# Gated cross-attention block on one core: the first projection of each attention unit in front of the denominators

## What is computed

```python
x = x + tanh(g_xattn[0]) * xattn(layernorm(x), ctx, w_q, w_k, w_v, w_o)
x = x + tanh(g_ffn[0])   * ffn(layernorm(x), gate_w, gate_up_w, down_w)

def xattn(query, kv, w_q, w_k, w_v, w_o):      # 16 heads of 8
    q, k, v = query @ w_q.T, kv @ w_k.T, kv @ w_v.T          # split into heads
    attn = softmax(einsum('bqhd,bkhd->bhqk', q, k) * 8 ** -0.5)
    return einsum('bhqk,bkhd->bqhd', attn, v) @ w_o.T

def ffn(x, gate_w, gate_up_w, down_w):         # 8 experts of 512, the best 2 of each token weighted
    ...
```

## Time and profile before

| | |
|---|---|
| three timed runs | 300.0, 299.88, 297.85 us, median 299.88 |
| profiled execution | 299.23 us |
| its span, first to last instruction | 297.5 us |
| PE busy | 284.7 us, 96% |
| DVE busy | 220.0 us, 74% |
| ACT busy | 181.3 us, 61% |
| POOL busy | 102.5 us, 34% |
| granted TensorE clock | 1.00 |

### The profile page before, as it was taken

The page is one execution under the profiler, slowest core; times in us unless marked ns, Lnnn a source line. Parts: engine busy times, 40 slices in busy tenths (PEclk is TensorE's granted clock), DMA queues, the critical chain, the costliest instruction groups (busy, mean ns, idle before and its releaser), DMA issues.

```text
span 297.5 us, 8034 instructions
## 1 busy us (share of the span) xinstructions
PE 284.7 (96%) x2826; PEld 218.9 (74%) x2826; DVE 220.0 (74%) x420; ACT 181.3 (61%) x370; POOL 102.5 (34%) x113
## 2 busy tenths in 40 slices
PE   7988999999999999999999999999889998998994
PEld 3464867876886886786787688887688887887862
DVE  4688878678786786777867878677256988888861
ACT  1635677676667757766767666557528775666500
POOL 4598423114015113312311411024500464776300
PEclk9999999999999999999999999999999999999999
DMA  7397960991792595298097079600000000000001
GB/s 249 88 203 196 220 194 16 209 249 54 162 264 96 103 218 197 52 220 248 0 218 198 0 156 240 237 0 2 2 2 0 1 2 0 0 1 0 0 0 31
DMA packets 9924, 32.19 MB, mean 108 GB/s; under 512 B 2576, under 2 KB 3088, under 8 KB 9904
## 3 DMA queue, kind: packets, MB, share of 16 engines
q1 hardware_dynamic: 9472, 31.60, 41.9%
q10 hardware_dynamic: 432, 0.33, 0.3%
HBM read 13.26 MB, written 0.23 MB: 45 GB/s over the span
## 4 chain that ended last, share of the span: by engine, by line
PE 86%; DVE 7%; issue 3%; ACT 2%; DMA 1%; SPq 0%; DVEq 0%; POOL 0%; ACTq 0%
PE score_ps L927 17%; PE max_ps L947 14%; PE o_ps L961 14%; PE misc_ps L915 7%; PE misc_ps L909 5%; PE score_ps L1190 3%; PE score_ps L1191 3%; PE score_ps L1192 3%; PE max_ps L977 3%; PE o_ps L1272 2%; PE misc_ps L999 2%; DVE part_max L687 2%; PE score_ps L909 2%; PE max_ps L970 1%; PE misc_ps L1106 1%
## 5 line engine op out<-in xcount | busy, mean ns | idle before, releaser
L687 DVE TENSOR_REDUCE part_max<-max_ps 112x1 f32<-112x512 f32 (+1 forms) x192 | 118.5, 670 | 40.4 <-PE max_ps L947 38.2
L510 ACT ACTIVATE probs<-score_ps 128x448 f32<-128x448 f32 x192 | 92.0, 543 | 28.9 <-PE score_ps L927 27.2
L947 PE MATMUL max_ps<-kx,qx 96*112 96x512 f32 (+1 forms) x192 | 77.5, 410 | 2.0 <-DVE part_max L687 0.9
L927 PEld LDWEIGHTS score_ps<-qx,kx 104*128 104x128 f32 (+1 forms) x384 | 66.5, 187 | 15.0 <-issue 7.9
L927 PE MATMUL score_ps<-qx,kx 104*128 104x224 f32 (+1 forms) x384 | 76.9, 285 | 0.5 <-ACT probs L510 0.4
L362 POOL TENSOR_TENSOR k_low<-k_full,k_high 128x512 fp32r<-128x512 f32 (+1 forms) x21 | 26.3, 1256 | 67.6 <-ACT k_full L493 67.3
L961 PE MATMUL o_ps<-probs,v_sb 128*32 128x112 f32 (+1 forms) x1536 | 47.6, 262 | 1.0 <-ACT probs L510 1.0
L961 PEld LDWEIGHTS o_ps<-probs,v_sb 128*32 128x32 f32 (+1 forms) x1536 | 36.1, 109 | 13.2 <-ACT probs L510 6.1
L947 PEld LDWEIGHTS max_ps<-kx,qx 96*112 96x112 f32 x192 | 33.8, 177 | 6.6 <-issue 2.9
L422 POOL TENSOR_TENSOR kx<-gu_sb,kx 128x512 fp32r<-128x512 f32 x16 | 23.0, 1440 | 30.6 <-ACT kx L590 30.4
L505 ACT ACTIVATE v_sb<-misc_ps 128x512 f32<-128x512 f32 x24 | 14.4, 601 | 20.0 <-PE misc_ps L915 20.0
(11 more groups left out here) (177 smaller groups left out, 376.7 us busy)
## 6 DMA issues: line engine op xcount, KB each, us to landing
kx<-k_high SPq DMA_DIRECT2D x60, 187.5 KB, 3.9
kx<-k_low SPq DMA_DIRECT2D x30, 187.5 KB, 3.9
ctx_sb<-in_ctxT SPq DMA_DIRECT2D x7, 750.0 KB, 6.1
gu_sb<-in_guT SPq DMA_DIRECT2D x8, 512.0 KB, 4.7
dn_sb<-in_dnT SPq DMA_DIRECT2D x8, 256.0 KB, 5.1
ctx_sb<-in_ctxT SPq DMA_DIRECT2D x2, 256.0 KB, 4.1
kx<-k_high SPq DMA_DIRECT2D x4, 123.5 KB, 2.3
kx<-k_high SPq DMA_DIRECT2D x4, 64.0 KB, 2.0
```

Source lines behind the costliest of these rows:

```text
L510: nc.scalar.activation(probs[:, (KT * h + t) % 8, :], score_ps[:, t % 3, 0:SC // 2], ACT.Exp, scale=SCALE).then_inc(exp_done, 1)
L687: nc.vector.reduce_max(part_max[:, p, c:c + 1], max_ps[0:PC, bank, 0:size], AX.X).then_inc(max_taken, turns)
L927: last = nc.tensor.matmul(score_ps[0:m, t % 3, GC * g:GC * g + GC], kx[0:KR, 2 * par + h, g, 128 * t:128 * t + m], qx[0:KR, par, 2 * h + g ...
L947: nc.tensor.matmul(max_ps[0:PC, bank, 0:size], qx[0:MR, par, 2 * h + p // 2, PC * (p % 2):PC * (p % 2) + PC], kx[0:MR, slot, p // 2, start ...
```

## The change

In each unit that goes through `attention` on TensorE, job 0 is issued ahead of the denominators, where it was issued behind them. Nothing else differs: the turns, banks, waits and the orders of the other engines stay.

```diff
                 scores(i, par, h, 3)
                 next_max(9, 3)
+                job(0)
                 denominators(u - 1, 1 - h, ring(u, RUN), RUN % 3)
-                job(0)
                 attend(i, par, h, 0)
```

## The result

| | before | after |
|---|---|---|
| median | 298.26 us (6 runs, 297.64 to 300.0) | 294.42 us (6 runs, 292.99 to 295.76) |
| ratio | | 0.9845, 95% interval 0.9807 to 0.9884 |
| profiled execution, its span | 299.23, 297.5 us | 295.45, 293.7 us |

The change made the kernel 1.6% faster, 3.8 us between the medians. Both kernels were run again later, beside the experiments; the changed one came out at 0.9832 (0.9788 to 0.9875) and 0.9846 (0.9804 to 0.9888) of before.

What follows compares the result with a forecast made beforehand. The prediction took TensorE as the bound, stopped in each unit by the denominators' wait for a bank. Savings of 12 x 0.30 + 0.37 + 0.35 = 4.3 us from 299.55 gave 295.3 us, range 293.9 to 298.4.

Steps and rivals of the forecast that it cites:

- two terms of the sum: From fourth maximum product to attend: projection 1.00 us (key unit 0.97), then denominators 0.22 us with their load hidden.
- the time that the saving is taken from: Whole kernel before the change: put at 299.55 us, the middle of the profiled 299.23 and the timed median 299.88.
- What bounds: TensorE, 96% busy, stands still 0.20 us a unit ahead of the denominators, whose bank VectorE's second reduction must leave.
- The wait goes and is not moved: Denominators behind the first projection: their bank is free 0.84 us before they come, so the wait disappears.
- The exposed load goes too: Denominators' first weight load, 0.09 us, goes in beneath the projection's last pass; they hold TensorE 0.22 instead of 0.31 us.
- the first rival: Denominators' weight load stays exposed behind the projection: saves only 3.0 us, giving 296.5 us; chance 0.14.
- The sum: Fourth maximum product to attend: 0.30 us saved in 12 loop units, 0.37 in unit 12, 0.35 in unit 13; 4.3 us.
- What is late next: Engines behind TensorE: VectorE's reciprocal starts at about 105.1, with 0.5 us idle left; nothing takes back the 0.30 us.
- The slower rival: Late reciprocal (L713) delays the fifth reduction and the transposed maxima in 14 units: 8.4 us lost, 303.7 us; chance 0.04.
- No effect: The 0.20 us gap belongs to the denominators and moves with them: 299.5 us; chance 0.12.
- half given back: Half the saving is lost to an unseen wait (maxima bank, exponentials or hand-written tail): 297.4 us; chance 0.08.

Runs made afterwards that it cites:

- the short reductions: Kernel before, old order, with VectorE's reductions of turns 0 and 1 reading only the first 256 columns; ratio 0.9872 to before.
- the filler: Kernel before, old order, with one unneeded matmul of the denominators' shape added ahead of the denominators in 14 units; ratio 1.0002 to before.
- the half swaps: Kernel before with job 0 ahead of the denominators only in units with h = 0 (ratio 0.9934), or only in those with h = 1 (0.9928).
- the kernel with unit 14 edited: Changed kernel with the denominators of hand-written unit 14 also moved, behind the fifth tile's scores; ratio 0.9825 to before.

## Which steps of the prediction held, and which failed

- **The step that failed: two terms of the sum.** The prediction had the denominators hold TensorE 0.22 us behind a projection, with their load hidden, and the projection 1.00 us. Measured are 0.31 and 0.89 (in a key unit 0.30 and 0.86, where 0.22 and 0.97 were put). The two errors nearly cancel, so the sum came out; the bullet on the exposed load says why they had to.
- **The other term that was off: the time that the saving is taken from.** It was put at 299.55 us, from three executions and the profiled one; the median of six is 298.26, so it was 1.3 us too high. The medians moved by 3.8 us and not by 4.3. These two misses point in opposite directions, and that the forecast of 295.3 lies only 0.9 us above the measured 294.42 is in part luck.
- **What bounds.** TensorE, stopped at one point in each unit by the bank of turn 1. Shown by the short reductions (the stall goes, in the old order) and by the filler (it costs nothing).
- **The wait goes and is not moved.** Shown: 0.86 to 0.90 us from the projection to the denominators in every unit of the changed order, the low clock of unit 0 apart, which is the projection's own passes. The sign that was given for it, the wait gone from the list, did not come: it is named 6 times, without cost.
- **The exposed load goes too.** Right in the sum, wrong in the place and in the test that I gave. Projection and denominators together take 1.20 us to attend (102.66 to 103.86); I had put 1.00 + 0.22. But the parts are 0.89 and 0.31. Of the 1.00 us between a projection and attend, 0.11 must be attend's own load of weights. It is exposed behind either neighbour: behind the denominators now (103.85 for a matmul at 103.86), and behind the projection in the kernel before:

```profile
105.12 0.73 PEld L961 LDWEIGHTS o_ps<-probs,v_sb 128*32 128x32 f32 x32
105.12 0.97 PE L961 MATMUL o_ps<-probs,v_sb 128*32 128x112 f32 x32
```

The old order with short reductions agrees, with the denominators at 0.20 us ahead of a projection, and 1.00 from the projection to attend. By the test as it was written ("with 0.31 the first rival is right") the reader would have decided for the rival. The distance to look at was the sum, or the load's row: 103.44 for a matmul at 103.55. The rule of the Trainium skill ("TensorE: Matmul & The Clock Gate", Part 3, "The mechanism"), that a load overlaps only in another row group, did not hold here either: all 128 rows on both sides, and the load went in beneath the projection (in unit 7 at 114.88, for a matmul at 115.31); an earlier sentence of that section, which also lets a load go ahead into a background weight buffer, fits these rows.
- **The sum.** 4.3 us predicted; the 14 steps measure 4.6. The saving of a loop unit was put a little small, 0.30 for 0.32. Between the medians it is 3.8 us in the first comparison, and by the three ratios 4.6 to 5.0.
- **What is late next.** The reciprocal was put at about 105.1 on unit 6's old clock; it started at 103.96 + 0.94 = 104.90. VectorE's idle time behind it was put at 0.5 and is 0.69 us.
- **The slower rival.** It has the mechanism right, and this is the part that was mis-sized: I gave the transposed maxima 0.28 us of room, from 108.63 to 108.91, and there are some 0.04; and the bank of turn 8, where the larger part is paid, was no part of that rival. Once the reduction of turn 5 is 0.3 us late, the whole of it is paid.
- **No effect** (the gap belongs to the denominators) and **half given back**: excluded by the short reductions and by the half swaps.

## What to carry to other kernels

Where an in-order engine passes work to a slower one through a few buffers, count at which turn of a burst the buffers run out, and put there a piece of work that uses no buffer of that ring. A stall also costs the weight load that could have gone in beneath the work ahead, so it is worth more than its idle time (here 0.11 us on top of 0.20). Then read how far the consumer falls behind: one place further back, this gain was gone.

The time between an end on one engine and the start that it releases on another is not room; take it off before a gap is called slack. Here it was 0.05 us from a reduction to the denominators' load, and 0.21 us from the last small step to that of the transposed maxima (108.04 to 108.25, in the kernel with the denominators behind attend).

## What the runs showed that was not expected

**A stretch of half the clock in the first unit.** In 7 of 13 profiles the granted clock of TensorE was at 1.2 instead of 2.4 GHz for 3.4 us, from between 29.1 and 30.1 us on. From the changed kernel's first profile:

```profile
28.00:30.00 2.00, 1.47 (x7) 1.33 (x8) 1.42 (x3) 1.02 (x2) 1.94 (x2) 0.78 0.95 197
30.00:32.00 2.00, 2.00 (x10) 1.84 (x9) 1.72 (x3) 1.09 (x2) 2.00 (x1) 0.50 0.94 195
32.00:34.00 2.00, 2.00 (x40) 1.72 (x40) 0.86 (x2) 0.60 (x1) 0.93 (x2) 0.86 0.99 238
```

(Stretch, its length, busy time of PE, PEld, DVE, ACT and POOL, granted clock, DMA share, GB/s.) In the third profile of the same kernel the clock is 1.00 in all three rows. Before it fell TensorE did the same list of work in both, and it fell ahead of the first instruction that the change moves. It costs the first profile of the changed kernel 1.3 us up to unit 1 and the second 1.4 (43.32 and 43.46 against 42.02), and in the executions of before the median of those with a mean clock of 0.994 or less lies 1.1 to 1.2 us above that of the others, in each of the three series. What decides whether it comes was not found.

**One expert that takes 1.1 us longer.** Behind the attention, from the first matmul of the experts to the store, the profiles have either 71.1 to 71.2 us (4 of 13) or 72.2 to 72.4 (9 of 13), with nothing between, though nothing there was edited. In the third profile of the changed kernel, which has the longer time, TensorE stands for VectorE (L845) in front of a gate's product twice, 1.5 us together; in the kernel with unit 14 edited, which has the shorter, once, 0.8 us. All three profiles of the changed kernel and both of before have the longer time, so it does not touch the comparison of these spans; but spans of the variants can't be subtracted without it, which is why the distances of the units stand in the table. Whether it belongs to a program or to an execution was not settled. In the last series eight executions of before at a mean clock of 1.00 took from 297.66 to 299.37 us, and the profiled one beside them, which has the longer time, 299.33; that looks like an execution's, but no profile of a short one of before was taken.
